# Sums over four key blocks instead of two, and the values of the second attention stage for eight heads at a time

## The reference

```
x = x + 0.5 * ffn0(layernorm(x)); x = x + attn0(layernorm(x)); x = x + 0.5 * ffn0(layernorm(x))
x = x + 0.5 * ffn1(layernorm(x)); x = x + attn1(layernorm(x)); x = x + 0.5 * ffn1(layernorm(x))
# either attention, 16 heads of 32 channels, causal:
att = softmax(where(causal, q @ k.T / sqrt(32), -inf));  y = att @ v;  out = y @ Wo
# attn0: 4 key/value heads shared by 16 query heads, biases, a position factor on q and k
# attn1: 16 key/value heads, no biases
```

## Time and profile before

| what | us |
|---|---|
| median of 3 runs | 2639.78 (2636.49 to 2643.28) |
| the profiled execution | 2630.22, its span 2628.5 |
| PE busy | 2530.7 (96%) |
| DVE busy | 1528.6 (58%) |
| ACT busy | 1045.8 (40%) |
| POOL busy | 966.4 (37%) |

### The profile page before, as it was taken

The page is one execution under the profiler, slowest core; times in us unless marked ns, Lnnn a source line. Parts: engine busy times, 40 slices in busy tenths (PEclk is TensorE's granted clock), DMA queues, the critical chain, the costliest instruction groups (busy, mean ns, idle before and its releaser), DMA issues.

```text
span 2628.5 us, 44135 instructions
## 1 busy us (share of the span) xinstructions
PE 2530.7 (96%) x16928; PEld 2010.6 (76%) x16928; DVE 1528.6 (58%) x3356; ACT 1045.8 (40%) x1901; POOL 966.4 (37%) x1357
## 2 busy tenths in 40 slices
PE   6999989989999999999999999999999899999999
PEld 4788867667668888888888878777777678888887
DVE  7777579979975445433333345798589643333333
ACT  7555346655653223311111133566466431111111
POOL 3333566766644225211111122666366521111110
PEclk9999999999999999999999999999999999999999
DMA  4222031132220110100000002342133100000001
GB/s 148 73 73 73 31 83 46 51 72 61 50 90 1 37 45 14 36 25 25 24 25 25 24 17 58 92 97 73 48 93 78 38 33 25 24 25 25 25 16 64
DMA packets 72002, 128.73 MB, mean 49 GB/s; under 512 B 15728, under 2 KB 24944, under 8 KB 71792
## 3 DMA queue, kind: packets, MB, share of 16 engines
q1 hardware_dynamic: 71792, 125.92, 16.9%
HBM read 62.42 MB, written 13.63 MB: 29 GB/s over the span
## 4 chain that ended last, share of the span: by engine, by line
PE 80%; DVE 8%; ACT 2%; POOL 2%; SPq 2%; DMA 2%; issue 2%; DVEq 0%; ACTq 0%; POOLq 0%
PE psum L1045 65%; PE psum L1163 4%; PE psum L1126 4%; PE psum L1144 4%; DVE psum L1495 2%; PE psum L1174 2%; SPq L1726 1%; PE psum L1054 1%; DVE s1a0rden L1534 1%; SPq L1745 1%; DVE s4a1rden L1534 1%; ACT s1a0e L1329 0%; DVE stats L1361 0%; POOL rstd L1604 0%; PE psum L1133 0%
## 5 line engine op out<-in xcount | busy, mean ns | idle before, releaser
L1495 DVE CUSTOM_DVE_ANT_0 psum<-psum,mask_q 128x512 f32<-128x512 f32 (+5 forms) x768 | 413.3, 575 | 100.0 <-PE psum L1126 97.0
L1045 PE MATMUL psum<-hA_hi,wmem 128*128 128x256 f32 (+1 forms) x1536 | 405.5, 334 | 0.5 <-DVE s1a0negmax L1495 0.3
L1045 PEld LDWEIGHTS psum<-hA_hi,wmem 128*128 128x128 f32 x1536 | 270.3, 191 | 32.0 <-DVE s1a0negmax L1495 1.5
L1045 PE MATMUL psum<-hA_lo,wmem 128*128 128x512 f32 (+1 forms) x864 | 293.8, 340 | 0.0
L1329 ACT ACTIVATE s4a1e<-psum,p_scale 128x384 f32<-128x384 f32 (+5 forms) x384 | 205.1, 579 | 92.2 <-PE psum L1144 88.8
L1448 DVE SCALAR_TENSOR_TENSOR x<-psum,x 128x512 f32<-128x512 f32 x256 | 175.8, 689 | 97.2 <-PE psum L1045 93.8
L1329 ACT ACTIVATE s1a0e<-psum,p_scale 128x384 f32<-128x384 f32 (+5 forms) x384 | 201.9, 577 | 76.3 <-PE psum L1144 74.9
L1419 DVE TENSOR_TENSOR s5f1prod<-psum,s5f1silu 128x512 f32<-128x512 f32 x64 | 44.3, 692 | 302.1 <-PE psum L1045 302.1
L1419 DVE TENSOR_TENSOR s3f1prod<-psum,s3f1silu 128x512 f32<-128x512 f32 x64 | 44.3, 692 | 294.1 <-PE psum L1045 294.1
L1616 POOL TENSOR_TENSOR wmem<-raw,wmem 128x512 fp32r<-128x512 f32 x58 | 74.2, 1289 | 314.8 <-ACT wmem L1231 314.7
L1045 PE MATMUL psum<-s3f1w,s3f1a 128*128 128x512 f32 x768 | 181.5, 390 | 0.9 <-POOL s3f1w L1616 0.9
(11 more groups left out here) (194 smaller groups left out, 5568.3 us busy)
## 6 DMA issues: line engine op xcount, KB each, us to landing
s1a0qst<-s1a0qs SPq DMA_DIRECT2D x96, 128.0 KB, 2.4
s4a1qst<-s4a1qs SPq DMA_DIRECT2D x96, 128.0 KB, 2.4
s4a1kst<-s4a1ks SPq DMA_DIRECT2D x96, 128.0 KB, 2.4
raw<-in_gate SPq DMA_DIRECT2D x44, 256.0 KB, 2.9
raw<-in_up SPq DMA_DIRECT2D x44, 256.0 KB, 2.8
raw<-in_down SPq DMA_DIRECT2D x44, 256.0 KB, 2.8
rounded<-s0f0w SPq DMA_DIRECT2D x24, 256.0 KB, 2.0
s2f0w<-rounded SPq DMA_DIRECT2D x24, 256.0 KB, 4.8
```

What stands on the lines that cost most here:

```text
L1045: ins = pe.matmul(out_, w, m, start=n == 0, stop=n == len(terms) - 1)
L1495: dve.tensor_tensor_reduce(scores, scores, mask_q[:, first:first + pw], -1.0, -MASKED, ALU.add, ALU.min, T[s]["negmax"][n % 2][:, column:c ...
```

## The change

- `den` only at the first of every four blocks. POOL makes one more sum (`e_sum`): the strip of block 2 (of 6), which already holds two, is added to that of block 0 (of 4): 768 and 256 columns a head. v of block 2 (6) is kept as the difference from block 0 (4), one more DVE subtraction. `pv` and `den` wait for the `e_sum` of their four blocks, and for its values' last difference (`v_dif`).
- The ring of exponentials grows from 7680 to 10240 (a0) and 10752 columns (a1), and a strip is freed when the last of its four blocks is done.
- a1: v for eight heads at a time: 32 `v_tile` of 12 products of 256 columns in four sets. The first set stands ahead of head 0, the others in groups 1, 3 and 5 from unit 14, one in two units; their weights (2 pieces a set) use slot 1 of `wmem`; q and k weights share slot 0, and those of group 1 are loaded behind group 0's projections.
- `TMPS` 4; `ln_norm` 4 units behind the statistics; `O_W_AT` 31; in stage 0 `ln_norm` is done by POOL.

```diff
-O_W_AT = 23
+O_W_AT = 31
-LN_AFTER = (0, 3, 6, 7, 8)
+LN_AFTER = (0, 4, 6, 7, 8)
-TMPS = 2
+TMPS = 4
+V_AT = 14
+V_STEP = 2
+V_W_AT = 4
-E32 = 7680
+E32 = {"a0": 10240, "a1": 10752}
...
-            put(values(1), HEADS * ST + (PV_LAG + 1) // 2 * 2 - 8, 1)
+            for vp in range(1, BATCH * HALVES):
+                put(v_weights_of(s, vp), (2 * vp - 1) * UNITS + V_W_AT, 2)
+                put(values(vp), (2 * vp - 1) * UNITS + V_AT, V_STEP)
...
-            if jt % 2 == 0:
-                plan.append(("den", s, n, k))
-                return
-            if k == PAIRS - 1:
+            if jt % HPG == 0:
+                plan.append(("den", s, n, jt // HPG))
+            if jt == ST - 1:
...
             if i % 2:
                 plan.append(("e_add", s, n, i // 2))
+            if i % HPG == HPG - 1:
+                plan.append(("e_sum", s, n, i // HPG))
...
-                name = ("v_out", "v_dif")[jt % 2]
-                on.wait_ge(sem[name], at(name, "v_out", s, n // HEADS, v_of(s, jt)))
-                on.wait_ge(sem["e_add"], at("e_add", "e_add", s, n, jt // 2))
+                on.wait_ge(sem["v_dif"], at("v_dif", "v_out", s, *v_of(s, n, jt)))
+                on.wait_ge(sem["e_sum"], at("e_sum", "e_sum", s, n, jt // HPG))
...
+                if tiles.stop % HPG:
+                    return
+                on.wait_ge(sem["v_odd"], at("v_odd", "v_out", s, b, t))
+                dve.tensor_tensor(v[:, tiles.stop - 2, :, :], v[:, tiles.stop - 2, :, :],
+                                  v[:, tiles.stop - HPG, :, :],
                                   ALU.subtract).then_inc(sem["v_dif"], 1)
...
+            def ln_norm(s, t):
+                if not normed_by_pool(s):
+                    return
...
+                pool.tensor_scalar(tmp[k % TMPS][:], x[:, t, :], rstd[:, t:t + 1],
+                                   shift[:, t:t + 1], ALU.mult,
+                                   ALU.add).then_inc(sem["ln_nm"], 1)
...
+            def e_sum(s, n, k):
+                begin, end = e32_place[s, n, HPG * k]
+                more, more_end = e32_place[s, n, HPG * k + 2]
+                e32 = T[s]["e32"]
+                on.wait_ge(sem["e_add"], at("e_add", "e_add", s, n, 2 * k + 1))
+                pool.tensor_tensor(e32[:, begin + 2 * P:end], e32[:, begin + 2 * P:end],
+                                   e32[:, more:more_end], ALU.add).then_inc(sem["e_sum"], 1)
```

More of the change, by code:

```diff
@@ L168, in group_weights, with v_weights_of @@
         return [split(s, n, g, 0) for n in names_of_group(s, g)]
+    def v_weights_of(s, vp):
+        return [split(s, "v", vp, i) for i in range(2)]
     def first_weights(s):
@@ L259, in attention @@
         v_weights = Beside(plan)
-        v_weights.waiting += [split(s, "v", 0, k) for k in range(1 if grouped else KT)]
+        v_weights.waiting += [split(s, "v", 0, 0)] if grouped else []
         def group_jobs(g):
@@ L302, in attention @@
         side = Beside(plan)
+        if not grouped:
+            for job in group_weights(s, 1):
+                side.start(job)
         side.waiting += values(0)
@@ L372, in attention @@
                 plan.append(("e_add", s, n, i // 2))
+            if i % HPG == HPG - 1:
+                plan.append(("e_sum", s, n, i // HPG))
             behind.append((n, i))
-            if len(behind) > PV_LAG and i % 2 == 1:
-                times_v(*behind.pop(0))
-                times_v(*behind.pop(0))
+            if len(behind) > pv_lag and i % pv_by == pv_by - 1:
+                for _ in range(pv_by):
+                    times_v(*behind.pop(0))
             for job in beside.pop(u, []):
@@ L426 @@
     "key": ("s_k", "exp"), "e_mask": ("e_mask",), "pv": ("pv",),
-    "e_add": ("e_add",), "den": ("den",), "y_fin": ("y_rec", "y_fin"),
+    "e_add": ("e_add",), "e_sum": ("e_sum",), "den": ("den",), "y_fin": ("y_rec", "y_fin"),
     "y_hi": ("y_hi",), "y_lo": ("y_lo",), "oproj": ("o_proj",), "x_sum": ("x_add",),
@@ L507, in run @@
         elif kind == "ln_norm":
-            done["norm", s, where[0]] = work("act", 0.81, ("stats", s, where[0]))
+            done["norm", s, where[0]] = work("pool" if s == 0 else "act", 1.3 if s == 0 else 0.81,
+                                             ("stats", s, where[0]))
         elif kind == "ln_tp":
@@ L547, in run @@
         elif kind == "v_tile":
[L548 removed]
+            done[step] = work("pe", 1.4, *banks)
         elif kind == "v_chunk":
@@ L573, in run @@
         elif kind == "e_add":
-            done["sum", s, *where] = work("pool", (SEQ - (2 * where[1] + 1) * P) / 400)
+            done[step] = work("pool", (SEQ - (2 * where[1] + 1) * P) / 400)
+        elif kind == "e_sum":
+            done["sum", s, *where] = work("pool", (SEQ - (HPG * where[1] + 2) * P) / 400)
         elif kind == "e_mask":
@@ L577, in run @@
         elif kind in ("pv", "den"):
-            width = SEQ - where[1] * P * (1 + (kind == "den"))
+            width = SEQ - where[1] * P * (HPG if kind == "den" else 1)
             done[step] = work("pe", width / 2400 + 0.1,
                               ("key", s, *where, 0 if width <= CH else 1),
-                              ("sum", s, where[0], where[1] // 2), *banks)
+                              ("sum", s, where[0], where[1] // (1 if kind == "den" else HPG)),
+                              *banks)
         elif kind == "y_fin":
@@ L858, in w_place @@
             if name in "qk":
-                return [wmem[:, g % 2, 2 * "qk".index(name) + p, :] for p in range(2)]
+                slot = g % 2 if STAGES[s] == "a0" else 0
+                return [wmem[:, slot, 2 * "qk".index(name) + p, :] for p in range(2)]
             if name == "v":
-                return [q[:, i, :] for q in T[s]["vw"]]
+                return [wmem[:, 1, 2 * p + i, :] for p in range(2)] if STAGES[s] == "a1" else \
+                    [q[:] for q in T[s]["vw"]]
             return [q[:] for q in T[s]["o_w"]]
@@ L1663, in gpsimd_program @@
             steps = {"begin": begin, "open": open_, "ln_stats": ln_stats, "w_split": w_split,
-                     "down": down, "e_add": e_add, "k_ones": k_ones, "bias_x": bias_x,
+                     "down": down, "ln_norm": ln_norm, "e_add": e_add, "e_sum": e_sum, "k_ones": k_ones, "bias_x": bias_x,
                      "e_mask": e_mask}
```

122 lines of the change are left out of this document (75 added, 47 removed).

## The result

The changed kernel takes 2660.94 us (2658.01 to 2661.58, four runs), the kernel before 2638.14 (2634.01 to 2643.28, four runs beside them): ratio 1.0081, 95% interval 1.0068 to 1.0094. That is **22.8 us slower**. The forecast was 2637, its range ended at 2650, and "slower" had the smallest chance. The profiled execution is one of 2660.87 us, its span 2659.1; against the one of before, 2630.22, it is 30.6 us longer, because the latter was among the fastest of its kernel. The heads are compared in these two executions, the kernels by their medians.

The account below looks back on a forecast made before the run. PE, 80% of the chain, was taken as the bound, with DVE or POOL as close in places. Terms from -15 for `den` to added POOL costs summed to -2.4 us: 2627.8 from the profiled execution, 2637 as median, range 2622 to 2650.

Parts of the forecast that it names:

- The saving: Both attention stages: half of the `den` steps, 28.2 us of PE time, go; -7 in a0, -8 in a1.
- The side edits: Value products of a1 +1.8 and -1, norms at the start -1.5, row buffers and longer ring -0.5.
- a sign that the forecast fails: Value products' new places in a1, or weights in one slot, make PE wait; or the start gives over 4 us.
- the one that hid the sums: Steady part: POOL's new sums, 2.58 us a head, fit its waiting time before `pv`, so they cost nothing there.
- two places of it: Group 4 of a0, with bias adds, +2.5; groups 2 and 6, with layer norms, +2 for both stages.
- Group 0 of a0: Start of a0: POOL, with bias adds and new sums, makes PE late by the third `pv`; +5.5 us.
- The ends: Last head of each stage: its two new sums stand in the chain; +2.5 in a0, +1.3 in a1.
- POOL becomes the bound of a0: Rival, 0.20: POOL can't be busy beyond about 87% in a0; a0 +12, a1 +3, kernel 2648 us.
- PE's waits on line 1721 all through a0: Sign for the rival that POOL bounds a0: PE waits for the `e_sum` sums throughout that stage.
- POOL's backlog is absorbed: Rival, 0.22: stops in groups 0 and 4 are half, 22 of 28.2 us of `den` come back; 2625 us.
- DVE takes a0's gain: Rival, 0.10: POOL's sums hold two-input DVE instructions in a0, whose gain of 7 shrinks to 2; +5, 2642 us.

Follow-up runs that it names:

- e1: Kernel before, with the second and fourth `den` of every head left out and nothing put on POOL: 2623.86 us, -15.5 against the kernel before.
- e3: Changed kernel with sums over two blocks as before (no `e_sum`, no third difference of v), all other edits kept: 2637.77 us, -1.6 against the kernel before.
- e2: Changed kernel with `e_sum` over 8 columns instead of 768 and 256, all waits kept: 2632.81 us, -6.5 against the kernel before.
- e14: Changed kernel with `e_sum` over 8 columns in heads 0 to 2, 30 and 31 of each stage, whole in the other 27: 2648.88 us.
- e13: Changed kernel with 70 useless products on PE ahead of the first `pv` of heads 1 and 31 in a0, 30 and 31 in a1: 2661.54 us.
- e6: Changed kernel with `row_min` as a reduction over one SBUF input instead of an operation with two: 2657.23 us, 4.4 less than the changed kernel.
- e7: Kernel before with `row_min` as a reduction over one SBUF input: 2637.93 us, -0.9 against the kernel before.

## Why the prediction was wrong

**The saving held.** -15 for the `den` taken off PE: -15.5 (e1).

**The side edits held as a sum,** -1.2 against -1.6 (e3). Not by each term: I had counted the load of group 1's weights at nothing; SP issued it behind 24 stack copies, the split that waits for it stood ahead of `v_out` on ACT, and PE had 10.8 us without work. The text had named this as a sign that the forecast fails. That the sum came out all the same, -1.2 for -1.6, is luck: the earlier start of a0 and others paid it back (e3). The step missed was to follow the moved load past each queue that it now stands behind.

**The step that failed is the one that hid the sums.** It reads: "`pv` comes nine units behind; the five units between are 7.9 us (12.7 x 5/8), and POOL's 78.7 us of waiting in 28 heads are 2.8 a head, just the new work." It put the sums in the steady part at nothing, beside 2.5 and 2 for two places of it. Measured: 16 us for the 27 inner heads of the two stages (e2 less e14, and 15.6 in the traces). The second half of the sentence put the wait for the fourth block at nothing as well; with sums of 8 columns the kernel is still 10 to 11 us behind the sum of its parts (e2). Both are in the 39.9 us that the sums over four cost in place of 13.8.

Why the step fails is in part a reading. Both of its numbers are means over heads, and the heads alternate: 9.9 and 14.7 us, in the last group 10.5, 7.3, 4.4. POOL's waiting lies in the long ones and can't be used in the short ones, whose 9.9 us are below its new floor of 10.3. That it is late at the ends is shown by its rows; in the steady part POOL still idles 24.9 us for ACT's exponentials, so it catches up there, and the lateness reaches PE by way of ACT and DVE, if that is its way. From "just the new work" I should have concluded that nothing is left over anywhere, and set a price on the steady part.

**Group 0 of a0** was right in kind and somewhat small: 5.5 against 8.5, by two stops of 3.85 and 3.53 us, at head 0's second and head 1's first four blocks, a head earlier than I had them. **The ends** were right in kind and too small: 2.5 and 1.3 against 5.0 and 6.4. I added the last head's two sums, as if POOL came to that head on time. It came late from the heads ahead: it is busy with hardly a break from 738 us on, and in a1 four splits of the next stage's weights, about 1.25 us each, stand in the same chain. I also left out that PE falls to its lower clock behind such a stop, about 2.0 and 2.5 us of the two (e13).

**The rivals.** *POOL becomes the bound of a0* was the right one, at 0.20, with 2648. What it put at an 87% limit for a0 as a whole: POOL now has 332.07 of 383.48 there, 86.6%. It gave a0 +12, where 18 were measured from the first row to the last `pv`, and a1 +3, where it was 7.6 from head 0 to head 31 and 6.5 ahead of that. Its sign, PE's waits on line 1721 all through a0, did not come: there are four, at the two ends of the stage. The slower time came out as it had it; by which way it comes in the steady part isn't shown. *POOL's backlog is absorbed* fell. *DVE takes a0's gain* was right on the hold and had no support for its price of 5 us: e6 gave 4.4, within its error, and e7 0.9. I had given the forecast more chance than the row it stood on could bear: need and room of POOL were equal, 2.6 and 2.8, and in such a case the late side is the likelier.

**Still open.** By which instruction the 16 us of the inner heads reach PE: it has next to no wait on line 1721 there, most of its own are short ones on ACT's exponentials, and in a0 the chain has moved to DVE's row maxima. And how much of the 19 us of lower clock is paid: among the 70 runs of the kernel before, the four at a mean clock of 0.994 have a mean span of 2632.2 us and the nine at 0.989 one of 2642.2, so there the time goes with it, though which causes which isn't shown; in the changed kernel about 4.5 us are paid at the two ends, and none in group 0 (e13).

## What to carry to other kernels

When work moves to an engine with a third of its time free, don't compare means: add up that engine's own time for one unit of work, its floor, and count the units that are now shorter than that. They show where to put a price; here they explain the ends, and not yet the whole of the steady part. A stop that is filled with useless work regains the clock, and time only if the engine that was waited for doesn't set the pace behind it. Of a load that is moved, look for the first instruction that waits for it on an in-order engine, and for what stands behind that.

## What the runs showed of the hardware

- A DVE operation on 4 columns with two SBUF inputs took 161 to 2044 ns beside POOL's sums; as a reduction over 8 columns, with one SBUF input, 161 to 166 in all 32 of a0. POOL's sum of 768 columns took up to 2.70 us in place of 1.87 while DVE had an operation with two SBUF inputs.
- An elementwise sum of 768 columns took POOL 1.87 us on average and DVE 1.02, of 256 columns 0.74 and 0.42; one of 8 columns still took POOL 0.21.
- After a stop of PE of 3.5 us eight products took 1.08 us instead of 0.64; with the stop filled by sixteen bf16 products, 0.64.
- The spread between runs of one kernel goes with the granted clock: a mean span of 2632.2 us at 0.994, of 2642.2 at 0.989, the same program.
- SP issued 24 copies one behind the other in 15.4 us, about 0.6 us each.
